# A graph network layer: edge features stored as one part, turned once, and the high part taken off in the PSUM bank

## Reference

```python
src, dst = edge_index[0], edge_index[1]
edge_emb = edge_attr @ W_edge + b_edge           # (40000,128) @ (128,512)
msg = relu(node_feats[src] + edge_emb)
aggr = segment_sum(msg, dst, num_segments=N)
h = (1.0 + eps) * node_feats + aggr
```

## Time and profile before

| what | value |
|---|---|
| median of 3 runs (lowest, highest) | 2767.33 us (2766.34, 2772.32) |
| the profiled execution: its time | 2766.0 us |
| the profiled execution: span, mean granted clock | 2764.2 us, 0.952 |
| busy PE / DVE / ACT / POOL over the span | 90% / 76% / 60% / 44% |
| message stage in the trace | from 1926.7 us (first turn) to about 2447 us |
| `features_dram` stores | 88 of 512 KB, median 3.0 us to landing |
| `edge_got` loads | 88 of 512 KB, median 5.3 us to landing |

### The profile page before, as it was taken

How to read it: one execution, slowest core, us unless ns; L and a number is a source line. 1 busy time by engine, 2 the same in 40 slices (tenths; PEclk the granted TensorE clock), 3 DMA queues, 4 the chain that set the end, 5 groups by cost and what they waited for, 6 DMA issues and landing times. The chain is left out here.

```text
span 2764.2 us, 45250 instructions
## 1 busy us (share of the span) xinstructions
PE 2479.7 (90%) x12847; PEld 1931.7 (70%) x12847; DVE 2096.7 (76%) x4088; ACT 1649.2 (60%) x3672; POOL 1219.8 (44%) x1214
## 2 busy tenths in 40 slices
PE   6999699999988999987999998688999999986887
PEld 3577355555477999946899996357788888865776
DVE  9898688888734898845388885566899999966667
ACT  1499688884223787712277773141888888835460
POOL 1777100003502766660077775423777777700211
PEclk9999899999988999998999999899999999998999
DMA  2220000004244555332455543513888888821101
GB/s 89 72 51 3 11 0 0 0 0 126 99 157 118 148 139 145 103 106 94 138 139 140 148 133 80 134 48 106 278 279 283 280 283 276 249 80 45 66 1 45
DMA packets 122480, 324.23 MB, mean 117 GB/s; under 512 B 24295, under 2 KB 38570, under 8 KB 122350
## 3 DMA queue, kind: packets, MB, share of 16 engines
q0 software_dynamic: 57216, 161.86, 19.8%
q1 hardware_dynamic: 65134, 160.72, 18.0%
HBM read 231.87 MB, written 82.51 MB: 114 GB/s over the span
## 5 line engine op out<-in xcount | busy, mean ns | idle before, releaser
L1842 POOL DMA_INDIRECT x_got<-table_dram,src_idx x352 | 374.9, 1065 | 120.5 <-issue 85.3
L725 POOL DMA_INDIRECT feature_rows<-in_edge_attr,ids x352 | 345.6, 982 | 110.0 <-issue 101.2
L676 ACT ACTIVATE hot_rest<-hot_dst,slot_w 128x128 bf16<-128x128 bf16 x864 | 272.7, 400 | 73.5 <-DVE hot_dst L630 68.6
L1281 DVE TENSOR_TENSOR pt_low<-bank,pt_high 128x640 fp32r<-128x640 f32 x320 | 263.0, 822 | 53.2 <-ACT pt_high L1244 51.9
L728 POOL COPY ids<-id_idx 128x32 uint32<-128x32 uint32 (+1 forms) x5 | 1.2, 240 | 666.3 <-DVE id_idx L843 371.1
L1244 ACT CAST pt_high<-bank 128x640 fp32r<-128x640 f32 x320 | 220.4, 689 | 115.5 <-PE bank L1195 115.4
L1972 DVE TENSOR_TENSOR msg<-bank,x_got 128x512 f32<-128x512 f32 x352 | 237.0, 684 | 59.6 <-PE bank L1867 47.8
L1275 DVE CUSTOM_DVE_ANT_0 p<-bank,log_counts 128x1254 f32<-128x1254 f32 x160 | 232.8, 1455 | 15.9 <-PE bank L1178 15.8
L1921 ACT ACTIVATE msg_high<-msg 128x512 fp32r<-128x512 f32 x308 | 193.6, 629 | 64.1 <-DVE msg L1972 64.0
L1195 PE MATMUL bank<-ident,p 128*128 128x128 f32 x1600 | 228.9, 275 | 2.3 <-DVE pt_low L1281 2.3
L1236 ACT ACTIVATE p<-p,bound 128x1254 f32<-128x1254 f32 x160 | 215.6, 1347 | 10.4 <-DVE bound L1275 10.4
(11 more groups left out here) (412 smaller groups left out, 6498.7 us busy)
## 6 DMA issues: line engine op xcount, KB each, us to landing
features_dram<-feature_parts POOLq DMA_DIRECT2D x88, 512.0 KB, 3.0
edge_got<-features_dram SPq DMA_DIRECT2D x88, 512.0 KB, 5.3
qk_dram<-qk_high SPq DMA_DIRECT2D x16, 640.0 KB, 2.9
qk_dram<-qk_low SPq DMA_DIRECT2D x16, 640.0 KB, 4.2
keys<-qk_dram SPq DMA_DIRECT2D x32, 320.0 KB, 4.7
queries<-qk_dram SPq DMA_DIRECT2D x32, 320.0 KB, 7.0
queries_low<-qk_dram SPq DMA_DIRECT2D x32, 320.0 KB, 9.1
acc_a<-zeros SPq DMA_DIRECT2D x1, 6400.0 KB, 31.6
```

Of the source, the lines that this page charges most:

```text
L676: last = act.activation(hot_rest[:, u, j, q, :], hot_dst[:, u, :, j], ACT.Copy, scale=k.slot_w[:, 1 + q, bass.ds(tile0 + j, 1)])
L725: pool.indirect_dma_start(out=rows[:, g % 2, j * ED:(j + 1) * ED], out_offset=None, in_=self.a.edge_attr_128, in_offset=bass.IndirectOffse ...
L1281: dve.tensor_tensor(p_low[:, made % 3, :, columns], unit(2 * n + u).rearrange("p (j n) -> p j n", n=P), p_high[:, made % 3, :, columns].bi ...
L1842: pool.indirect_dma_start(out=xg[:, g % XRING, j, :], out_offset=None, in_=k.table_dram, in_offset=bass.IndirectOffsetOnAxis(ap=k.src_idx[ ...
```

## The change

1. POOL no longer splits the features: the gathered rows are stored as they are (256 KB per group in place of 512 KB). With no `parts` buffer between, the wait for the store of the group before now stands ahead of the next group's loads.
2. SP loads 256 KB per group into a ring of four buffers (`ERING`) in place of two.
3. PE `turn` is four transposes of float32 (`is_transpose`) in place of eight fast matmuls, into one bank (0 or 1, by turns), whose accumulation is left open. ACT copies it with rounding (`copy_high`). PE `take_off` then multiplies that high part by minus the identity into the same bank, so the bank holds the low part, and ACT copies it (`copy_low`).
4. On ACT `copy_high(s+2)` stands behind `relu(s)` where `copy_turned(s+2)` stood; `copy_low(s+1)` stands inside `relu(s)`, behind its first Relu and the one-hot matrix.
5. PE's step is `turn(s+2)`, `embed(s+1)`, `take_off(s+2)`, `collect(s)`; two steps stand ahead of the loop, whose body holds four.

```diff
@@ class Features: places, gather
-        self.parts = r.take("feature_parts" + where, [P, 2, GT * ED], F32R)
...
         for g in range(first, first + groups):
             u = g % 2
+            if g > first:
+                gate(pool, self.saved, of(16 * g, 16 * LAYER_GROUPS), self.passed)
             if g + 1 < first + groups:
                 load(g + 1)
             gate(pool, self.got[u], of(16 * GT * (g // 2 + 1), 16 * GT * LAYER_GROUPS // 2), self.passed)
-            if g > first:
-                gate(pool, self.saved, of(16 * g, 16 * LAYER_GROUPS), self.passed)
-            pool.tensor_copy(parts[:, 0, :], rows[:, u, :]).then_inc(self.made, 1)
-            gate(pool, self.made, of(2 * g + 1, 2 * LAYER_GROUPS), self.passed)
-            pool.tensor_tensor(parts[:, 1, :], rows[:, u, :], parts[:, 0, :].bitcast(F32), ALU.subtract).then_inc(self.made, 1)
-            gate(pool, self.made, of(2 * g + 2, 2 * LAYER_GROUPS), self.passed)
-            pool.dma_start(k.features_dram[bass.ds(of(g, LAYER_GROUPS), 1), :, :].rearrange("g p n -> (g p) n"),
-                           parts[:].rearrange("p q n -> p (q n)").bitcast(F32)).then_inc(self.saved, 16)
+            pool.dma_start(k.features_dram[bass.ds(of(g, LAYER_GROUPS), 1), :, :].rearrange("g p n -> (g p) n"), rows[:, u, :]).then_inc(self.saved, 16)
@@ edge_messages: SP
-                    sp.wait_ge(turned_e, (i * 2 + u) * 2 - 2)
-                    messages.load(sp, i, u)
+                    sp.wait_ge(turned_e, i * ERING + g - ERING + 1)
+                    messages.load(sp, i * ERING + g, g % ERING)
@@ edge_messages: PE
-                if not first:
-                    pe.wait_ge(e_copied, (i * 2 + u) * 2)
-                pe.wait_ge(got_e[u], i * 16 + 16)
-                for q in range(2):
-                    for j in range(GT):
-                        t = pe.matmul(k.bank[:, q, j * P:(j + 1) * P], ea[:, u, q, j, :], ident_r[:], start=True, stop=True)
-                    t.then_inc(turned_e, 1)
+                for j in range(GT):
+                    t = pe.matmul(k.bank[:, u, j * P:(j + 1) * P], ea[:, r, j, :], k.ident[:], is_transpose=True, start=(j == 0), stop=False,
+                                  skip_group_check=True)
+                t.then_inc(turned_e, 1)
+
+            def take_off(g, u):
+                pe.wait_ge(e_high, g + 1)
+                pe.matmul(k.bank[:, u, :], minus_r[:], et[:, u, 0, :], start=False, stop=True, skip_group_check=True).then_inc(e_rest, 1)
...
+            def step(s, n, pairs):
+                turn(s + 2, n + 2)
+                embed(s + 1, (n + 1) % 2)
+                take_off(s + 2, n % 2)
+                collect(s, n % 2, pairs)
@@ edge_messages: ACT
-                for q in range(2):
-                    act.wait_ge(turned_e, g * 2 + q + 1)
-                    act.copy(et[:, u, q, :], k.bank[:, q, :]).then_inc(e_copied, 1)
+                act.wait_ge(turned_e, g + 1)
+                act.copy(et[:, u, 0, :], k.bank[:, u, :]).then_inc(e_high, 1)
+
+            def copy_low(i, u):
+                g = i * 2 + u
+                act.wait_ge(e_rest, g + 1)
+                act.copy(et[:, u, 1, :], k.bank[:, u, :]).then_inc(e_low, 1)
...
                         act.activation(hot[:, u], distance[:, u], ACT.Relu, bias=one[:], scale=-1.0).then_inc(hot_ready, 1)
+                        if rest:
+                            copy_low(*rest)
```

More of the change, by code:

```diff
@@ L713, in places @@
         self.rows = r.take("feature_rows" + where, [P, 2, GT * ED], F32)
-        self.parts = r.take("feature_parts" + where, [P, 2, GT * ED], F32R)
     def gather(self, pool, first, groups, turn, l=None):
-        k, ids, rows, parts = self.k, self.ids, self.rows, self.parts
+        k, ids, rows = self.k, self.ids, self.rows
         def of(n, a_layer):
@@ L1601, in _ @@
                 if b == 4:
-                    for u in range(2):
-                        messages.load(sp, 0, u)
+                    for r in range(ERING):
+                        messages.load(sp, r, r)
                 sp.dma_start(raw[:, b % TILES], k.at_dram[b]).then_inc(at_loaded[b % TILES], 16)
@@ L1816, in edge_messages @@
     xg = r.take("x_got", [P, XRING, GT, D], F32)
[L1817 removed]
+    ea, w_high, w_low, minus_r, one = messages.ea, messages.w_high, messages.w_low, messages.minus_r, messages.one
     et = r.take("edge_turned", [P, 2, 2, GT * P], F32R)
@@ L1827, in _ @@
         def _(sp):
-            with sp.Fori(1, NG // 2) as i:
-                for u in range(2):
-                    sp.wait_ge(turned_e, (i * 2 + u) * 2 - 2)
-                    messages.load(sp, i, u)
+            for g in range(ERING, ERING + NG % ERING):
+                sp.wait_ge(turned_e, g - ERING + 1)
+                messages.load(sp, g, g % ERING)
+            with sp.Fori(0, (NG - ERING) // ERING) as i:
+                for v in range(ERING):
+                    g = NG % ERING + ERING + v
+                    sp.wait_ge(turned_e, i * ERING + g - ERING + 1)
+                    messages.load(sp, i * ERING + g, g % ERING)
         @block.gpsimd
@@ L1867, in embed, with collect @@
                     pe.matmul(to, et[:, u, 1, at], w_high[:], start=False, stop=True).then_inc(emb_done, 1)
-            def collect(i, u):
-                g = i * 2 + u
+            def collect(g, u, pairs):
                 pe.wait_ge(hot_ready, g + 1)
@@ L1882, in collect, with copy_high @@
                 m.then_inc(summed, 1)
+            def step(s, n, pairs):
[3 more added lines that the diff above has]
+                collect(s, n % 2, pairs)
             pe.wait_ge(messages.w_split, 3)
-            turn(0, 0, True)
-            turn(0, 1)
+            for g in range(2):
+                turn(g, g)
+                take_off(g, g)
             embed(0, 0)
-            with pe.Fori(0, NG // 2 - 1) as i:
-                turn(i + 1, 0)
-                embed(i, 1)
-                collect(i, 0)
-                turn(i + 1, 1)
-                embed(i + 1, 0)
-                collect(i, 1)
-            embed(NG // 2 - 1, 1)
-            collect(NG // 2 - 1, 0)
-            collect(NG // 2 - 1, 1)
+            lead = (NG - 2) % ERING
+            for s in range(lead):
+                step(s, s, s // 2)
+            with pe.Fori(0, (NG - 2) // ERING) as i:
+                for v in range(ERING):
+                    n = lead + v
+                    step(i * ERING + n, n, i * (ERING // 2) + n // 2)
+            embed(NG - 1, 1)
+            collect(NG - 2, 0, NG // 2 - 1)
+            collect(NG - 1, 1, NG // 2 - 1)
         @block.scalar
         def _(act):
-            def copy_turned(i, u, first=False):
+            def copy_high(i, u, first=False):
                 g = i * 2 + u
@@ L1931, in _ @@
                 apart_from(0, 0, j)
-            copy_turned(0, 0, True)
-            copy_turned(0, 1, True)
+            copy_high(0, 0, True)
+            copy_low(0, 0)
+            copy_high(0, 1, True)
+            copy_low(0, 1)
             relu(0, 0, True)
-            copy_turned(1, 0)
-            relu(0, 1, True)
-            copy_turned(1, 1)
+            copy_high(1, 0)
+            relu(0, 1, True, rest=(1, 0))
+            copy_high(1, 1)
             with act.Fori(1, NG // 2 - 1) as i:
-                relu(i, 0)
-                copy_turned(i + 1, 0)
-                relu(i, 1)
-                copy_turned(i + 1, 1)
-            relu(NG // 2 - 1, 0)
+                relu(i, 0, rest=(i, 1))
+                copy_high(i + 1, 0)
+                relu(i, 1, rest=(i + 1, 0))
+                copy_high(i + 1, 1)
+            relu(NG // 2 - 1, 0, rest=(NG // 2 - 1, 1))
             relu(NG // 2 - 1, 1, last=True)
```

35 lines of the change are left out of this document (18 added, 17 removed).

## The result

The changed kernel takes 2743.57 us (median of 4 runs, 2739.29 to 2746.36); the kernel before, run beside it, 2769.82. The ratio is 0.9904, with a 95% interval of 0.9882 to 0.9925. That is 26.3 us faster, where 19 were forecast; as a time it lies 4.4 us under the 2748 forecast and inside the range. The profiled execution took 2741.97 us, with a span of 2740.3 against 2764.2 before.

A forecast was written before the change was run, and what follows sets the result against it. PE's instructions were taken to pace the message stage; 16 us from its steps plus 3 from the `edge_got` waits made 19, so 2766.0 − 19 = 2747 profiled and 2748 as median. Its own range was 2743 to 2753, the stated range 2741 to 2761.

The forecast's parts named there:

- What bounds the stage: Message stage: PE's instructions pace it, 5.74 us a step, until another engine does.
- Turn: PE's step in the message stage: transposes and `take_off` cost 0.71 us against 0.90; 0.19 a step, 16.0 us over 84.
- Ring of four: End of the message stage: two PE waits for `edge_got` go, gaining 3.0 us, at the other end 0.
- Gather: Layer 0 and `finish_layer`: nothing; attention: cycles of 8.0 us plus 25 for late landings, ending within the block.
- Sum: Whole kernel: 16 + 3 = 19 us gained, 2747 for the profiled execution, 2748 as median.
- Copies on ACT: ACT in the message stage: same number of copies, only their lateness changes; no cost while ACT keeps its cover.
- The fill: Message stage, DVE's 11.7 us wait for the first gathered rows: a gain of 0 to 3 us, taken as 0.
- POOL "5.46, narrow": POOL in the message stage: four indirect DMAs a group take 5.46 us against a new step of 5.55.
- POOL's wait for DVE mostly gone: Sign in the message stage: POOL's 32.1 us of waiting for DVE would mostly go.
- The rivals: POOL paces 0.13; gather ends attention 0.08; ACT-PE ring 0.05; transposes at record length 0.01; nothing gained 0.03; more gained 0.04.
- The gather ending the attention blocks: Attention in two layers: from a mean cycle of 9.4 us, gather ends 3 to 12 us late; 2760 us; chance 0.08.

The follow-up runs named there:

- e5: Changed kernel with the subtracting matmul `take_off` issued twice: 2757.34 us.
- e4: Changed kernel with `take_off` run on 16 of its 512 columns: 2736.04 us.
- e6: Changed kernel with four float32r matmuls of 128 columns in place of the four float32 transposes: 2744.15 us.
- e3: Changed kernel with the ring of `edge_got` buffers back to two (`ERING = 2`): 2744.6 us.
- e11: Kernel before, with source rows of empty slots spread (own partition number instead of row 0): 2764.28 us, ratio 0.9981 to the kernel before.
- a0: Changed kernel measured again, unaltered, with more rounds: 2743.11 us, ratio 0.9903 to the kernel before.
- e10: Changed kernel with source rows of empty slots spread (own partition number instead of row 0): 2737.76 us, ratio 0.9871 to the kernel before.
- e2: Changed kernel with the old gather (copy, subtraction, 512 KB stores), the message stage reading the first half of each stored row: 2748.67 us.
- e7: Changed kernel with `take_off` ahead of the last of the four embedding tiles: 2746.84 us, ratio 0.9903 to the kernel before.
- e1: Kernel before with the change's gather alone, its load reading the 256 KB twice: 2766.24 us, ratio 0.9989 to the kernel before.
- e9: Changed kernel whose gather stores each group's rows twice, 512 KB, without GpSimd work on them: 2795.82 us.
- e8: Changed kernel with GpSimd's copy and subtraction back, into a tile nobody reads, ahead of the 256 KB store: 2902.82 us.

## Why the prediction was right, and where it was not

**What bounds the stage: right.** PE paces it before and after. e5 lengthened the step by the whole matmul, e4 shortened it by all that PE gave up.

**Turn: right in mechanism, a little small.** 0.22 a step was gained, not 0.19. The four transposes took 0.35, where 0.39 stood in the sum; 84 × 0.22 = 18.2 us, not 16.0. The 275 ns that the prediction quotes from the Trainium skill (TensorE: Matmul & The Clock Gate, Part 4: PE-mode transpose) are not what a transpose in a row of them costs: the next kind of matmul starts 0.35 us behind the first of four, and e6 shows fast matmuls of that size no cheaper.

**Ring of four, 3.0 us: the step of the prediction that failed.** It read two waits for `edge_got` as the ring's and the load's own, and their end as time gained. The halved load does end them, with a ring of two as well (e3). But e11 has the old ring and the old load and no such wait either: what made the loads late were the gathers that read one row 128 times. These are still there in the changed kernel, where they show as waits of DVE for `x_got` instead (1.90 us in the profiled run, 7.5 in a0's). From the first `collect` to the end of the last one, spread rows take 4.1 us off the kernel before (e11) and 6.6 off the changed kernel (e10). So the end of the stage lost 2.5 us by the change, where 3.0 were to be gained.

**Gather, "I put it at nothing" for layer 0 and finish_layer: failed.** The forecast looked only for who waited for the gather, not for whom its vector work slowed. It is worth 5.6 us (e2 against a0), about 3 in each finish_layer: this is most of what the forecast was short of. In the profiled execution the first of the two hardly showed it (197.6 to 197.0), in a0 it did (194.7). DVE's instructions are as fast in both (936 and 932 ns for the 1251 columns); what differs is the clock at the start: in the first 10 us of the stretch PE is granted 0.50 and 0.60 of full speed in the changed kernel's profile, 0.67 and 1.00 in a0's, and 0.64 and 1.00 before. e4, e5, e7 and e10 are like the former (197.0 to 197.2), e1, e3 and e6 like the latter (194.4 to 194.7); what decides it stays open. For attention the arithmetic held: a usual cycle of 8.0 us forecast, 7.9 found; 25 us for late landings, 27 found (31 × the 0.88 by which the mean of 8.81 is above the median of 7.93); the last store issued at 1161.25, some 17 us ahead of the block's end.

**Sum.** Forecast 16 + 3 = 19. Of the 23.9 us between the two spans 17.0 are in the stage (about 19.5 from its steps, less 2.5 at its end) and 3.7 in the two finish_layer stretches (5.8 in a0); the remaining 3.2 are small differences elsewhere that no run takes apart. Two terms missed in opposite directions and partly cancelled, the ring by −5.5 and the gather by +4 to +6. That the time came out only 4.4 us under 2748 is in part luck: the gain was 7.3 us larger than forecast, but the kernel before, run beside it, stood 2.5 us above the 2767.33 that the forecast started from.

**Copies on ACT at nothing: right.** e7 took 20 us of ACT's waits away and won nothing. At a step of 5.40 (e4) the ring between ACT and PE still held. The fill at nothing was right too: DVE's 11.7 us became 11.6.

**POOL "5.46, narrow": too high.** It counted 0.30 of issue at each indirect DMA. The row itself has (374.9 + 85.3) / 88 = 5.23 a group, since no issue time stands where POOL waited for DVE; in e4 it is (365.1 + 87.8) / 88 = 5.15, and POOL still waits for DVE at a step of 5.40. What an indirect DMA takes depends on DVE's low part (two inputs in SBUF) more finely than the 1.46 or 0.95 of the prediction: between 2000 and 2380 of the changed kernel it is 0.94 to 0.95 us when it starts outside one, 1.14 to 1.28 with 0.3 to 0.4 us of one left, and 1.44 to 1.46 with 0.6 left. In the forecast's list "POOL's wait for DVE mostly gone" was wrong: 32.1 us became 25.3.

**The rivals.** None of them happened. The gather ending the attention blocks was nearer than its 0.08 suggests for small edits: e9, with 0.8 us more in a usual cycle and 1.2 more in the mean, lost 28 us in one such block.

## What to carry to other kernels

Work on GpSimd for which nobody waits is not free: look at the mean length of DVE's instructions beside it, and at the clock PE is granted behind the wait that they lengthen. Before a wait at the end of a stage is put down to the ring or the bytes of the transfer it names, look at what else is in the DMA engines then; an indirect gather whose empty entries all point at one row lands late and takes its neighbours with it. When a store is moved ahead of the loads that reuse its buffer, add up the cycle, with its late landings, and compare it with the stage's end at once; here a mean cycle of 8.8 us cost nothing and one of 10.0 some 50 us.

## What the hardware showed that was not expected

- Indirect DMAs that read the same 2 KB row 128 times land in 9.2 us (changed kernel) and 10.0 us (before), in ten other runs 8.9 to 13.2; with distinct rows in 3.6 (e10) and 4.6 (e11). These are medians of the last 11 to 25 of the stage, with the DMA engines shared with the rest of it.
- A float32 transpose of 128 columns and a float32r matmul of 128 columns cost PE the same: four of either and the change to 512 columns take 0.67 and 0.68 us.
- A matmul of 16 columns gives back 0.09 of the 0.21 us that it saves to the matmul behind it.
- A 128x1 instruction of DVE (0.16 us) that started inside a copy or subtraction of GpSimd took 0.58 and 1.06 us: it ended 0.01 to 0.02 us behind that copy or subtraction.
- A wait of PE of 4.2 us was followed by 10 us with a granted clock of 0.82 and 0.84 (before), one of 3.6 us by 8 us at 0.72 and 0.85 (e8), one of 2.7 us by full clock in the changed kernel and by 4 us at 0.66 in e9.
